# Cross-attention on one Trainium2 core: normalising x on VectorE instead of ScalarE

## The reference

```
x = x + self_attention(layernorm(x))
x = x + cross_attention(layernorm(x), ctx, ctx, gamma)     # the stage that is changed
x = x + expert_mix(layernorm(x))

layernorm(x) = (x - mean(x)) / sqrt(var(x) + eps)
cross_attention: q, k, v of shape (16, 256, 512); 8 heads of 32 rows:
    gamma * einsum(softmax(einsum(q, k) / sqrt(32)), v)
```

## Time and profile before

| | us |
|---|---|
| median of three runs | 2922.05 |
| lowest and highest of them | 2916.3, 2922.57 |
| the profiled execution | 2915.57 |
| span in its trace | 2913.9 |

### The profile page before, as it was taken

The page is one execution under the profiler, slowest core; times in us unless marked ns, Lnnn a source line. Parts: engine busy times, 40 slices in busy tenths (PEclk is TensorE's granted clock), DMA queues, the critical chain, the costliest instruction groups (busy, mean ns, idle before and its releaser), DMA issues. The chain is left out here.

```text
span 2913.9 us, 40038 instructions
## 1 busy us (share of the span) xinstructions
PE 2703.7 (93%) x13726; PEld 2042.1 (70%) x13726; DVE 1800.4 (62%) x3515; ACT 1032.8 (35%) x2543; POOL 948.0 (33%) x786
## 2 busy tenths in 40 slices
PE   3699999999999999999999999995999999979873
PEld 2588888888888888888888888884444444439752
DVE  7466556655655566656665666654776776633588
ACT  3222222332222322222232222222577777753321
POOL 2111111421111222211132111112578887760263
PEclk9999999999999999999999999998899999985697
DMA  8421112321221223211232113103776677610003
GB/s 313 170 78 68 58 58 96 122 73 58 73 102 58 91 69 116 73 58 58 87 130 73 58 59 114 60 30 121 183 189 193 175 186 185 186 41 0 0 0 115
DMA packets 165202, 289.98 MB, mean 100 GB/s; under 512 B 11680, under 2 KB 78240, under 8 KB 162976
## 3 DMA queue, kind: packets, MB, share of 16 engines
q1 hardware_dynamic: 165024, 287.66, 31.5%
HBM read 194.81 MB, written 92.27 MB: 99 GB/s over the span
## 5 line engine op out<-in xcount | busy, mean ns | idle before, releaser
L439 PE MATMUL pj<-xnt,whi 128*128 128x512 f32 x2048 | 704.2, 405 | 15.8 <-DMA xnt<-xt_scratch 15.8
L519 ACT ACTIVATE pr<-sc,nmx 128x128 f32<-128x128 f32 (+1 forms) x512 | 210.6, 416 | 934.3 <-DVE nmx L591 934.3
L394 POOL TENSOR_TENSOR qt<-rot,swp 128x512 f32<-128x512 f32 x128 | 166.1, 1298 | 1126.5 <-DVE swp L572 1126.5
L439 PEld LDWEIGHTS pj<-xnt,whi 128*128 128x128 f32 x2048 | 385.7, 188 | 108.0 <-DMA xnt<-xt_scratch 16.2
L990 DVE TENSOR_REDUCE xnmx<-xsc 128x1 f32<-128x512 f32 x512 | 336.7, 685 | 163.6 <-PE xsc L810 160.7
L439 PE MATMUL pj<-xnt,wlo 128*128 128x512 f32 x1024 | 398.8, 389 | 0.0
L780 POOL TENSOR_TENSOR xprt<-xprt 128x512 f32<-128x512 f32 x256 | 320.2, 1280 | 116.3 <-PE xob L830 63.2
L436 PE MATMUL pj<-whi,xnt 128*128 128x512 f32 x1024 | 351.7, 405 | 0.0
L932 ACT ACTIVATE xprt<-xst 128x512 f32<-128x512 f32 x512 | 290.7, 595 | 112.5 <-PE xst L819 109.1
L570 DVE TENSOR_TENSOR rot<-pj,trig 128x512 f32<-128x512 f32 x256 | 177.0, 691 | 226.3 <-PE pj L439 226.3
L591 DVE TENSOR_REDUCE nmx<-sc 128x1 f32<-128x128 f32 (+1 forms) x512 | 158.6, 352 | 177.4 <-PE sc L465 172.9
(11 more groups left out here) (155 smaller groups left out, 4615.6 us busy)
## 6 DMA issues: line engine op xcount, KB each, us to landing
xnt<-xt_scratch SPq DMA_DIRECT2D x64, 1024.0 KB, 8.0
x_scratch<-xio SPq DMA_DIRECT2D x64, 512.0 KB, 3.6
xio<-x_scratch SPq DMA_DIRECT2D x48, 512.0 KB, 4.1
qst<-sq_scratch SPq DMA_DIRECT2D x96, 256.0 KB, 5.0
kst<-sk_scratch SPq DMA_DIRECT2D x96, 256.0 KB, 5.7
xt_scratch<-parts SPq DMA_DIRECT2D x16, 1024.0 KB, 4.7
sq_scratch<-qp SPq DMA_DIRECT2D x32, 512.0 KB, 8.0
sk_scratch<-kp SPq DMA_DIRECT2D x32, 512.0 KB, 4.7
```

The lines of the kernel that those rows point to most:

```text
L394: nc.gpsimd.tensor_tensor(qk["QK".index(kind)][h][:, :, :].rearrange("p b n -> p (b n)"), rot[r % 2][:, :], swp[r % 2][:, :], ALU.add).the ...
L439: last = nc.tensor.matmul(bank[:, :], wpart[:, w, i * HD:(i + 1) * HD], moving, start=(k == 0), stop=(k == 3 * CB - 1))
L519: nc.scalar.activation(pr[:, a % 4, lo:hi], SC[a % 2][:, lo:hi], ACT.Exp, bias=nmx[:, a % 4, t:t + 1], accum_out=rsum[:, a % 4, t:t + 1]). ...
```

## The change

`normed` moves from ScalarE's stream to VectorE's. It is a tensor_scalar there, (x - mean) * rstd, with the mean and `rstd` as per-partition scalars, as in the first layer norm; `shift` and its semaphore go. Its place is (1, 0), that is behind the first maximum of step c = 1, where it was at (1, 1) in ScalarE's stream. Its two waits go with it, and it is still four tiles ahead. GpSimd's stream, TensorE's and SyncE's stay as they are.

```diff
-        shift = sb("shift2", [P, TILES], F32)
...
-        s_shift = sem("x_shift")
...
             rstd_of_all(nc, act, None, rstd, tmp, s_var, s_sqrt, s_step, scale=XSCALE)
             act.wait_ge(s_gam, 16)
-            act.wait_ge(s_shift, 1)
-
-            def normed(m):
-                act.wait_ge(s_xi[m % 6], 16 * (m // 6 + 1))
-                act.wait_ge(s_qlo, m)
-                nc.scalar.activation(xn[:, :], x2[:, m, :], ACT.Identity, scale=rstd[:, m:m + 1],
-                                     bias=shift[:, m:m + 1]).then_inc(s_qn, 1)
...
             WORK = {(0, 0): ((k_round, 3),), (0, 1): ((repeat, -2),), (0, 2): ((v_evac, 0),), (1, 0): ((output_evac, -1),),
-                    (1, 1): ((normed, 4),), (1, 3): ((q_round, 4),), (2, 2): ((max_round, 1),), (2, 3): ((sums_evac, -1),)}
+                    (1, 3): ((q_round, 4),), (2, 2): ((max_round, 1),), (2, 3): ((sums_evac, -1),)}
...
             rstd_of_all(nc, None, dve, rstd[:, :], tmp, s_var, s_sqrt, s_step, scale=XSCALE)
-            nc.vector.scalar_tensor_tensor(shift[:, :], mv2[:, :, 0], -1.0, rstd[:, :], ALU.mult, ALU.mult).then_inc(s_shift, 1)
+
+            def normed(m):
+                dve.wait_ge(s_xi[m % 6], 16 * (m // 6 + 1))
+                dve.wait_ge(s_qlo, m)
+                nc.vector.tensor_scalar(xn[:, :], x2[:, m, :], mv2[:, m, 0:1], rstd[:, m:m + 1],
+                                        ALU.subtract, ALU.mult).then_inc(s_qn, 1)
...
-            WORK = {(0, 1): ((statistics, -3),), (0, 2): ((mean_and_variance, -3),), (2, 0): ((output, -2),),
+            WORK = {(0, 1): ((statistics, -3),), (0, 2): ((mean_and_variance, -3),), (1, 0): ((normed, 4),), (2, 0): ((output, -2),),
                     (2, 2): ((max_rest, 1),), (3, 3): ((one_over_sums, -1),)}
```

## The result

The changed kernel takes 2924.06 us (median of 17 runs, 2921.96 to 2926.2), the kernel before, measured beside it, 2919.0 us (17 runs, 2915.49 to 2923.21). The ratio is 1.0016, 95% interval 1.0008 to 1.0023: 5 us, or 0.16%, slower. The profiled execution took 2922.38 us with a span of 2920.7, 6.8 us above the span of before.

What follows compares the result with a forecast made beforehand. TensorE was taken as the busiest engine, with VectorE's second maximum of c = 1 on its path. Terms 0.74 + 0.45 + 0.4 + 4.8 = 6.4 us gave 2928.4 us on the median; 8-in-10 range 2919 to 2940 us.

Steps and rivals of the forecast that it cites:

- my own bound of 0.2%: About 0.2% (5.8 us) is what a measurement of this kernel can tell from no change; the forecast sits on that edge.
- the start-up: Start of cross-attention: normalisation held by GpSimd's memset, first scores 0.74 us later; tile 3's normalisation 0.45, tile n = 0 0.4 us.
- The hold: VectorE's normalisation in c = 1 stands still until GpSimd's key remainder ends, then needs 0.27 us: 0.87 us instead of 0.54.
- The path through c = 1: In c = 1 the normalisation delays the second maximum, hence the fourth score matmul; step c = 2 starts 0.59 us late.
- The absorption: Late starts and mid-step waits of c = 2 hide part of the 0.59 us, leaving about 0.2 us per tile.
- The lower bound of 7.69 us for the stretch: First matmul of c = 1 to weighted sum of c = 2 takes at least 7.69 us; the mean before was 7.58.
- the 4.8 us of the sum: Tiles 1 to 27: lifting the twenty stretches below 7.69 us to that value adds 4.8 us in all.
- ScalarE's wait: ScalarE's idle time before rounding the queries, until a DMA write lands, grows by about 20 us; removing its work gains nothing.
- Not held or fully absorbed: VectorE is not held by GpSimd, or waits of c = 2 swallow it: 0 to 2 us, 2923 us; chance 0.22.
- Nothing absorbed: DMA waits move with TensorE, so 0.59 us adds up in all 27 tiles: 18 us, 2940 us; chance 0.20.
- Faster through ScalarE: ScalarE's queue, not the DMA, releases the exponentials of c = 2; removing 0.82 us in 28 tiles gives 2901 us; chance 0.08.

Runs made afterwards that it cites:

- the pair with the late rounding: Kernel before and changed kernel, each with ScalarE's query rounding moved behind the exponentials of c = 2: 2911.28 us (0.9971) and 2919.84 us (0.9998).
- The run with the late memsets: Changed kernel with GpSimd's three memsets of ones moved behind its first remainders: 2924.07 us, ratio 1.0015 to the kernel before.
- slot (1, 3): Changed kernel with the normalisation behind the last maximum of c = 1 instead of the first: 2918.99 us, ratio 0.9997 to the kernel before.

## Why the prediction was right, and where it was not

I forecast 2928.4 us, 6.4 us more than before; measured were 2924.06 us and 5.1 us more (0.16%), inside the range. Of the 4.3 us between the two times 3 are the median of the kernel before, which three runs had put too high, and 1.3 the change. By my own bound of 0.2% it ends on the "same" side of the edge I had put it on; but the interval, 1.0008 to 1.0023, does not contain 1, so with 17 runs that bound was too wide.

The sum came out closer than its terms: in the profiled executions the start-up was charged 1.5 us too high and the tiles 0.8 us too low. That these partly cancel is luck.

**The hold: right.** 0.936 us in the median (0.9 forecast), ending 0.29 us behind GpSimd's instruction (0.27). It is there in each of the tiles 1 to 27. Its cause is shown by the kernels in which GpSimd waits or the slot is another.

**The path through c = 1: right.** Fourth score matmul at 2.73 us on average over the tiles 1 to 27 (2.73 forecast), c = 2 at 4.40 (4.42).

**The absorption: right in kind, a little large.** The lower bound of 7.69 us for the stretch is what the tiles show: most are at 7.65 to 7.70, mean 7.81 because four tiles, with 8.27 to 8.67 us, had late DMAs. Only one of them, tile 7, is among the seven that were above 7.69 before, so the excess that I left as it was does not belong to fixed tiles. The steady part came to 5.6 us over 26 tiles of the profiled execution against the 4.8 us of the sum. That the waits in the middle of c = 2 absorb is shown by the pair with the late rounding, 8.6 us against 5.1; that the late start of c = 2 absorbs the larger part is read from the traces (0.31 us later on average, not 0.59).

**The start-up: wrong.** I charged 0.74 + 0.45 + 0.4 = 1.6 us; the 0.74 is for the first scores, the other two terms for what follows up to tile 1. The first normalisation was held as described, and for as long, but the stage reached its first scores no later (21.77 us against 21.88). The step that failed is "the write, the reads and the first scores come after it in a row": they do, but they do not start when the normalisation lets them. The run with the late memsets shows that not even 1.8 us at that place reach the scores: the writes land no sooner. From the first scores to tile 1 it took 0.16 us more, not 0.85. With -0.1 and 0.16 for these terms the sum is 4.9 us, next to the measured 5.1.

**ScalarE's wait: wrong, without effect.** I expected its idle time at the rounding to grow by 20 us; it went from 40.6 to 39.8 us. The freed time is in its wait for the transposed scores, 132.8 us against 104.7 before: the last score of c = 1 comes later, and the time is spent one instruction earlier in the same queue. That removing 26 us of work from ScalarE is worth nothing came out as forecast.

**The rivals.** Not held or fully absorbed (2923 us, 0 to 2 us more): not held is refuted by the durations, and the interval of the 5 us, 0.08% to 0.23% or 2.3 to 6.7 us, lies above 2. Nothing absorbed (2940 us, 18 us more): refuted by the time. Faster through ScalarE (2901 us): refuted by slot (1, 3), which has the relief without the hold and is at 0.9997.

**What stays open.** Holding the key remainder back by 1.4 us, with nothing else, gains 5 us (0.9983). The trace shows the key write (issued behind it) landing in 3.6 us in the median instead of 4.6, and the query write ahead of it in 7.9 instead of 8.0; the stretch to the weighted sum of c = 2 is shorter by only 0.04 us per tile. The profiled execution is the slowest of this kernel's eleven (2919.77 us against a median of 2914.6), so its trace does not show where the gain lies. That it is less collision among DMAs is argued, not shown. The comparison of the two kernels that this study is about is not touched by it, since neither has it.

## What to carry to other kernels

Before a tensor_scalar over fp32 in SBUF goes to VectorE, look at what GpSimd runs at that very place: the one waited for the other's whole instruction in every tile here, so the price is set by the length of GpSimd's pieces and by what is queued behind the instruction on VectorE, not by VectorE's busy share. The same instruction cost 5 us ahead of a maximum that a matmul waits for, and nothing measurable three places later, where GpSimd stands idle. A DMA wait in the middle of a queue is better placed behind the work that others wait for; it was worth more here (8 us) than the question of which engine normalises. And a start-up that waits for DMAs already issued does not get shorter because the instruction ahead of a write does.

## What the runs showed of the hardware

- A tensor_scalar of fp32 from SBUF to SBUF over 128x512 beside GpSimd ends 0.28 to 0.29 us after GpSimd's instruction, whether that is a tensor_tensor over 128x512 (0.90 us), one over 128x2048 (3.93 us) or a memset (1.84 us). Even one over 128x32 waits: 1.80 us, and 0.18 us without the memset. The form matters: beside the same memsets a tensor_tensor over 128x32 on VectorE (line 59) takes 0.19 us, as without them.
- Between two GpSimd instructions without a gap VectorE gets in, and then GpSimd is the one that waits (its second piece 1.46 us instead of 1.28).
- Maxima that read PSUM are not touched: 0.69 us beside GpSimd's instruction as elsewhere.
- One pair sum over 128x2048 takes GpSimd 4.55 us, four over 128x512 take 5.0 us.
- TensorE's granted clock went from 1.00 to 0.50 after it had stood still for 2.49 us in the kernel with the 128x2048 pair sums and after matmuls at 1.00 up to 2314.8; it is 0.50 from 2315 to 2318 and 1.00 again from 2318.6.
